# Sums of squares of keys and queries taken from the key-key diagonal and from transposed queries, and TensorE's wait for the key copies moved between the key-key and the key-query products

## The reference, cut to what matters

```python
def _rmsnorm(x, eps=EPS):
    return x * jax.lax.rsqrt(jnp.mean(x * x, axis=-1, keepdims=True) + eps)
...
q = _rmsnorm(q) * inv
k = _rmsnorm(k) * inv
...
M = jnp.where(stril, jnp.einsum('bhncd,bhnmd->bhncm', k_beta, k) * decay, 0.0)
T = solve_triangular(eye + M, eye, lower=True)
...
attn = jnp.einsum('bhcd,bhed->bhce', q_i, k_i) * dec_i
```

## Time and profile before

| | |
|---|---|
| runs | 3674.81, 3671.62, 3674.26 us; median 3674.26 us |
| profiled execution | 3675.09 us, span 3673.2 us, granted clock 0.98 |
| PE busy | 3349.1 us (91%), 18978 matmul records |
| DVE busy | 2456.2 us (67%) |
| ACT busy | 2027.6 us (55%) |
| POOL busy | 1597.0 us (43%) |

### The profile page before, as it was taken

How to read it: one execution, slowest core, us unless ns; L and a number is a source line. 1 busy time by engine, 2 the same in 40 slices (tenths; PEclk the granted TensorE clock), 3 DMA queues, 4 the chain that set the end, 5 groups by cost and what they waited for, 6 DMA issues and landing times. The chain is left out here.

```text
span 3673.2 us, 58820 instructions
## 1 busy us (share of the span) xinstructions
PE 3349.1 (91%) x18978; PEld 2623.9 (71%) x18978; DVE 2456.2 (67%) x5159; ACT 2027.6 (55%) x4826; POOL 1597.0 (43%) x2825
## 2 busy tenths in 40 slices
PE   0259999999999999999999999999999999999987
PEld 0247777777777777777777777777777777777763
DVE  7746676666767676766666676766666676766643
ACT  6734556555655556555655556555655555555531
POOL 7634534444443534444453534444453435444310
PEclk9979999999999999999999999999999999999988
DMA  3322222222222222222222222222222222222102
GB/s 118 122 57 56 83 76 77 55 78 76 66 60 78 81 78 72 60 78 75 66 61 78 81 76 62 73 77 74 68 61 78 81 72 61 78 76 68 46 8 103
DMA packets 295395, 265.78 MB, mean 72 GB/s; under 512 B 221584, under 2 KB 250384, under 8 KB 285840
## 3 DMA queue, kind: packets, MB, share of 16 engines
q1 hardware_dynamic: 286160, 131.99, 14.9%
q10 hardware_dynamic: 8928, 130.03, 9.6%
HBM read 232.30 MB, written 29.62 MB: 71 GB/s over the span
## 5 line engine op out<-in xcount | busy, mean ns | idle before, releaser
L688 PE MATMUL x<-xs,w_high 128*128 128x512 f32 x3072 | 1064.3, 428 | 23.0 <-POOL w_low L1325 13.9
L923 ACT ACTIVATE uvec<-rb,cpos 128x128 f32<-128x128 f32 x512 | 160.5, 365 | 870.0 <-PE rb L708 870.0
L688 PE MATMUL x<-xs,w_low 128*128 128x512 f32 x1536 | 613.2, 399 | 0.0
L688 PEld LDWEIGHTS x<-xs,w_high 128*128 128x128 f32 x3072 | 531.7, 193 | 87.6 <-POOL w_low L1325 14.4
L1000 ACT ACTIVATE slot<-lane 128x512 fp32r<-128x512 f32 x640 | 351.2, 610 | 295.9 <-PE lane L814 295.9
L1308 POOL TENSOR_TENSOR block_step<-block_in 64x14 f32<-64x14 f32 (+6 forms) x896 | 231.2, 258 | 338.1 <-DMA block_in<-blocks_dram 216.8
L688 PEld LDWEIGHTS x<-xs,w_low 128*128 128x128 f32 x1536 | 293.0, 191 | 67.6
L1365 POOL TENSOR_TENSOR rstd<-rarg,powers 128x8 f32<-128x8 f32 x64 | 106.1, 1657 | 530.9 <-DVE rarg L1116 530.9
L814 PEld LDWEIGHTS lane<-pinv,slot 128*128 128x128 f32 x1536 | 199.7, 192 | 190.2 <-ACT slot L1000 98.4
L1284 POOL TENSOR_TENSOR lower<-bt,offdiag 128x512 fp32r<-128x512 f32 x128 | 171.6, 1340 | 323.7 <-DVE bt L1160 323.7
L1079 DVE SCALAR_TENSOR_TENSOR cacc<-x,cwv,cacc 128x511 f32<-128x511 f32 (+2 forms) x384 | 281.7, 747 | 37.2 <-ACT cacc L910 2.8
(11 more groups left out here) (227 smaller groups left out, 7638.9 us busy)
## 6 DMA issues: line engine op xcount, KB each, us to landing
xs<-mix_dram ACTq DMA_DIRECT2D x62, 2048.0 KB, 7.7
gb<-cum_dram SPq DMA_DIRECT2D x128, 256.0 KB, 4.5
w_in<-in_w_qkvz SPq DMA_DIRECT2D x48, 512.0 KB, 4.1
w_out<-in_w_out SPq DMA_DIRECT2D x16, 512.0 KB, 4.5
blocks_dram<-bt SPq DMA_DIRECT2D x512, 8.0 KB, 1.5
inverse_dram<-block_out SPq DMA_DIRECT2D x64, 128.0 KB, 2.2
inv<-inverse_dram SPq DMA_DIRECT2D x512, 16.0 KB, 1.8
xacc<-in_x SPq DMA_DIRECT2D x4, 1024.0 KB, 10.6
```

The source lines that it names most:

```text
L688: ins = mm(PROJ_BANK[kind][i][:, :], w, x, start=(k == 0 and j == 0), stop=(k == KC - 1 and j == 2))
L923: ins = a(uvec[:, h, :], rb[:, sl(h, HD)], ACT.Copy, scale=sm2[p]["cpos"][:, ch, h:h + 1])
```

## The change

1. The 8 one-column matmuls of `key_sums` are gone from TensorE, and with them ScalarE's `squares_qk`. The line's place on TensorE has `query_tokens`: 4 transposes of the raw queries into x1.
2. The key sums are the diagonal of the key-key products: VectorE multiplies x0 by the identity (128x512) and reduces it along each chunk (`key_sums`), in slot 10.
3. ScalarE squares the transposed queries from x1 (`query_squares`, 128x512), between the copies of job 1 and job 2, and VectorE reduces them (`query_sums`), in slot 12 ahead of `small`. `small` reads both sums from a small SBUF tile.
4. `key_products` waits for `ktok_ready` only before the key-query products.
5. VectorE's two scans of the second mixing stage keep their place before the new `key_sums`.

```diff
-            def key_sums(l, m):
-
-                W("sq_ready", l + 1)
+            def query_tokens(l, m, p):
+
                 if m is not None:
                     W("z_ready", 2 * m + 1)
-                for i in range(2):
-                    for ch in range(NCH):
-                        ins = mm(x1[:, 4 * i + ch:4 * i + ch + 1], sq[:, i, sl(ch, CH)], t["ones"][:, :], start=True, stop=True)
-                ins.then_inc(S["sums_full"], 1)
+                for ch in range(NCH):
+                    ins = nc.tensor.transpose(x1[:, sl(ch, HD)], qkT2[p][:, 1, sl(ch, CH)], ident[:, :])
+                ins.then_inc(S["qtok_full"], 1)
 
             def key_products(l, m, p):
                 W("qk_ready", 2 * l + 2)
-                if m is not None:
-                    W("ktok_ready", m + 1)
                 for i, bank, name in ((0, x0, "kk_full"), (1, rc, "kq_products_full")):
+                    if i == 1 and m is not None:
+                        W("ktok_ready", m + 1)
                     for ch in range(NCH):
...
-            def squares_qk(p):
-                act.drain()
-                a(sq[:, :, :].rearrange("p i s -> p (i s)"), qkT2[p][:, :, :].rearrange("p i s -> p (i s)"), ACT.Square).then_inc(S["sq_ready"], 1)
+            def query_squares(l):
+                W("qtok_full", l + 1)
+                a(sq[:, 0, :], x1[:, :], ACT.Square).then_inc(S["squares_ready"], 1)
...
-                        elif k == 9:
-                            squares_qk(p)
+                        elif k == 10:
+                            query_squares(l)
...
+            def key_sums(l):
+
+                work = sq[:, 1, :].rearrange("p (c s) -> p c s", s=CH)
+                W("kk_full", l + 1)
+                v.tensor_tensor(work, x0[:, :].rearrange("p (c s) -> p c s", s=CH), ident[:, :].unsqueeze(1).to_broadcast([P, NCH, CH]), ALU.mult)
+                dve.drain()
+                v.tensor_reduce(sums[:, 0, :], work, AX.X, ALU.add)
+
+            def query_sums(l):
+
+                W("squares_ready", l + 1)
+                v.tensor_reduce(sums[:, 1, :], sq[:, 0, :].rearrange("p (c s) -> p c s", s=CH), AX.X, ALU.add)
+
             def small(m, p):
 
                 dve.drain()
-                W("sums_full", m + 1)
                 W("masked", 2 * m + 2)
-                v.tensor_scalar(skt[:, :], x1[:, 0:4], HD * EPS, None, ALU.add)
-                v.tensor_scalar(qe[p][:, :], x1[:, 4:8], HD * EPS, HD * EPS * HD * EPS, ALU.mult, ALU.add)
+                v.tensor_scalar(skt[:, :], sums[:, 0, :], HD * EPS, None, ALU.add)
+                v.tensor_scalar(qe[p][:, :], sums[:, 1, :], HD * EPS, HD * EPS * HD * EPS, ALU.mult, ALU.add)
...
+                        elif k == 10:
+                            if b == 1:
+                                mix_backward(*mix_unit(l))
+                            elif b == 2:
+                                mix_forward(*mix_unit(l))
+                            key_sums(l)
                         elif k == 12:
+                            query_sums(l)
                             small(l, p)
```

More of the change, by code:

```diff
@@ L528, in attention_phase @@
         sm2 = [{n: sb(f"{n}{i}", [P, NCH, HPG]) for n in ("egp", "egn", "edec", "egl", "cpos")} for i in range(2)]
+        sums = sb("sums", [P, 2, NCH])
         skt = sb("skt", [P, NCH])
@@ L539, in attention_phase @@
                  "v_tap0_ready qk_tap0_ready v_conv_done qk_conv_done v_ready qk_ready z_ready "
-                 "gathered block_in_loaded block_inverted block_stored inv16_loaded sq_ready sums_full sk_ready exps_ready irk_ready ktok_full ktok_ready kk_full kq_products_full vtok_full "
+                 "gathered block_in_loaded block_inverted block_stored inv16_loaded qtok_full squares_ready sk_ready exps_ready irk_ready ktok_full ktok_ready kk_full kq_products_full vtok_full "
                  "vtok_ready gneg_ready masked decay_ready b_ready lower_ready "
@@ L874, in body @@
                         if L:
-                            key_sums(l, m)
+                            query_tokens(l, m, p)
                         if B:
@@ L1262, in body @@
                             attention_weights(l, 1, p)
[L1263 to L1267, removed]
                     if B and k in (15, 16, 17):
```

## The result

The changed kernel takes 3527.5 us (median of 4 runs, 3526.5 to 3531.9) against 3673.8 us before (3671.6 to 3674.8). The ratio is 0.9605 with a 95% interval of 0.9588 to 0.9622: 3.9% faster.

A forecast was written before the change was run, and what follows sets the result against it. TensorE's queue was taken to bound the kernel. Gains of 0.73 and 1.36 us a body, limited by ScalarE to 1.85, made 114.7 us over 62 bodies: 3675.1 to 3560 us, 3.1% less, range 3540 to 3590.

The forecast's parts named there:

- What bounds the kernel: TensorE's queue sets the time: busy 2723 of 2800 us in the steady part, idle 1.4 of a 51.5 us body.
- The wait: On TensorE, key-key products no longer wait for ScalarE's key copies and start earlier: gain 0.73 us a body.
- The sums against the transposes: On TensorE, 16 records of one-column sums (1.76 us) give way to four transposes (0.40): gain 1.36 us a body.
- Rival C: Four transposes on TensorE don't overlap and take 1.08 us; a body gains 1.41, 3588 us; chance 0.12.
- ScalarE ahead of job 2: ScalarE's copies ahead of job 2 limit the gain to 1.85 us a body, 0.24 less than TensorE alone.
- The square: ScalarE's new 512-element square behind job 1's copies takes 0.6 us and costs nothing, covered by the half z projection.
- VectorE's: A product of 0.65 us and two reductions of 0.6 each, 1.9 us a body, all in VectorE's idle time.
- its room: VectorE's spare time ahead of the addition of job 4 after the added work: 1.5 us.
- the sum: 62 bodies at 1.85 us each, 114.7 us, taken from the profiled execution's 3675.1 us: 3560 us.

The follow-up runs named there:

- e1: Kernel before with only the wait for the key copies moved between the two key products: 3775.7 us, ratio 1.0279 to before.
- e2: Changed kernel with the wait for the key copies put back in front of both key products: 3565.6 us, ratio 0.9707 to before.
- e7: Changed kernel with ScalarE's square of the queries behind the copies of job 2 instead of ahead of them: 3533.7 us, ratio 0.9607 to before.
- e9: Changed kernel with four more VectorE reductions of the squared queries ahead of the one that counts: 3607.9 us, ratio 0.9827 to before.
- e3: Kernel before with the sums' eight matmuls 64 columns wide instead of one: 3647.9 us, ratio 0.9930 to before.
- e6: Kernel before with the key-copy wait moved between the key products and the sums' matmuls 64 columns wide: 3641.4 us, ratio 0.9905 to before.
- e5: Changed kernel with eight one-column matmuls added ahead of the query transposes and the key-copy wait back before both key products: 3729.4 us, ratio 1.0139 to before.
- e10: Changed kernel with eight 64-column matmuls added ahead of the query transposes and the key-copy wait back before both key products: 3681.0 us, ratio 1.0027 to before.
- e4: Changed kernel with eight one-column matmuls added ahead of the four query transposes: 3633.0 us, ratio 0.9891 to before.
- e8: Changed kernel with exp_decay split by head around ScalarE's copies of job 5, head 1's b_matrix behind job 6's addition: 3450.2 us, ratio 0.9381 to before.

## Why the prediction was right and wrong

**What bounds the kernel** held: TensorE's queue. Every edit that changed a body did so by what it took from TensorE or made it wait.

**The wait** was sized at 0.73 us; the key products now start 0.72 us earlier behind the projection. e1 shows what the prediction didn't work out: without the other half of the change this gain does not exist, since the wait goes to ScalarE's squares. The two halves are worth 0.15 and 1.3 us alone (e1, e2) in a body without a fall, and 1.9 together.

**The sums against the transposes** were sized at 1.36; measured 1.30 (0.46 for four transposes). Rival C is out: one transpose takes 281 ns in the mean, but the four overlap. By the Trainium skill's figure of about 275 ns (TensorE: Matmul & The Clock Gate, "Part 4: PE-mode transpose") the four would, as an estimate, have held TensorE for 1.1 us; the trace has the duration but not that distance.

**ScalarE ahead of job 2** was forecast to cost 0.24 us and cost about 0.2. A regular body was forecast 1.85 shorter and is 1.89 shorter. **The square** costs nothing (e7). **VectorE's** reductions were taken at 0.6 and measure 0.68 and 0.69, the second of them 0.75 to the start of `small` behind a drain (the prediction's price was somewhat low, and cost nothing); its room was 1.5 forecast and 1.7 to 1.9 in most bodies, and e9 shows that the room is real. The rule that a product with one input in PSUM is not held by GpSimd (Trainium skill, SBUF — State Buffer, "Who interferes with whom") is agreed with: the product took 0.68 at 1949.99, while GpSimd's weight split ran from 1949.12 for 3.18 us.

**The step that failed is the sum**: "62 bodies with all three thirds, 1.85 each: 114.7", taken from the profiled execution's time, with nothing for the clock. It treated that time as made of regular bodies. It was not: 13 of 63 bodies were about 1.5 us or more longer, 12 of them with a fall of the granted clock to half for 3.4 us and the last with one of 6.8, and these 22 us went with the change (the last body's 2 of them may belong with the end). The rows for it were in hand and not followed: the earlier trace rows has a clock of 1.00 in the body and 0.99 in the 2800 us, and 63 bodies of 51.51 don't make the distance between the first and the last. So the mechanism of a regular body was right, and the forecast lacked this term: the regular bodies brought 119 us for the 114.7 of the sum, the falls 22, the start and the end 1.9 and 5.8, which no run puts down to the change. Had the falls stayed, the measured 3527.5 would be 3549, inside the range.

**The cause of the falls** is shown in one part and less closely in the other. The width of the eight matmuls is shown: in three pairs of kernels with bodies of equal length (before and e3, e1 and e6, e5 and e10) 64 columns instead of one take 12, 55 and 27 falls away. That the idle time has a part rests on e4, which has the narrow matmuls without the wait and no fall, against e5, which has the wait back and 27. But the wait also makes e5's body 0.76 us longer, and no pair of equal length tests it by itself. The falls are 12 and 27 where the wait ends 2.7 us ahead of the narrow matmuls (before, e5), and 55 where it stands directly ahead of them (e1). Idle time of this size without narrow matmuls gives none (e2); the one fall of e9, behind 1.50 us of idle time and with no narrow matmul, says that a longer wait may be enough, from a single case.

The change removes both. To take the narrow matmuls away is enough (e2), and with them but without the wait there is no fall either (e4); but to move the wait in the kernel before is not, since it comes back ahead of the sums (e1). Why one body in five has a fall and the next four not, why e5 has twice as many as before, and what exactly ends them, stays open; no run here tells it.

## What to carry to other kernels

Before a sum is set against a measured time, divide the time into its repeats: list the lengths of the bodies and ask why some are longer, and take a granted clock of 0.99 as a row to follow. Eight matmuls of one column took as much time here as eight of 64 (a body of 51.5 us in both, e3), and next to a wait they cost the clock too; either make them wide or do the work elsewhere. Price idle time from start to start: the 0.72 us listed ahead of job 6 were 1.28 (e8). And a wait moved alone may land on the next producer: e1 made the kernel 2.8% slower with an edit that only lets TensorE start earlier.

## What was unexpected of the hardware

The granted clock fell 55 times in e1 and never in the same bodies of e6, with the same instructions in the same order, a body of 51.36 us in both, and 64 columns instead of one. Making matmuls 64 times wider, with the same results, made the kernel 0.7% faster (e3) and in the arrangement of e1 3.6% (3641.4 against 3775.7 us). A fall of 3.4 us makes a body about 1.5 us longer before (53.0 against 51.5) and 1.65 in e5 (53.6 against 51.9).
